# Routed rows in four classes instead of three, and the fourth lot of rows summed within the last three expert tiles

## What is computed

```python
xn = layernorm(x) * gamma + beta
logits = xn @ Wr + br                       # 8 experts
top_vals, top_idx = top_k(logits, 2)
w = softmax(top_vals)
for e in range(8):
    h = gelu(xn @ W1[e] + b1[e])            # 256 -> 512
    y += (h @ W2[e] + b2[e]) * w_full[:, e] # 512 -> 256
out = x + y
```

## Time and profile before

| what | value |
|---|---|
| median of three runs | 1207.3 us |
| lowest and highest of the three | 1204.22 and 1209.26 us |
| the profiled execution's own time | 1203.97 us |
| its span in the trace | 1202.2 us |
| PE busy | 1143.5 us, 95% of the span |
| DVE busy | 700.4 us, 58% |
| ACT busy | 418.6 us, 35% |
| POOL busy | 227.3 us, 19% |
| DMA | 105.98 MB, mean 88 GB/s |

### The profile page before, as it was taken

The page is one execution under the profiler, slowest core; times in us unless marked ns, Lnnn a source line. Parts: engine busy times, 40 slices in busy tenths (PEclk is TensorE's granted clock), DMA queues, the critical chain, the costliest instruction groups (busy, mean ns, idle before and its releaser), DMA issues.

```text
span 1202.2 us, 26290 instructions
## 1 busy us (share of the span) xinstructions
PE 1143.5 (95%) x7856; PEld 810.2 (67%) x7856; DVE 700.4 (58%) x1425; ACT 418.6 (35%) x806; POOL 227.3 (19%) x279
## 2 busy tenths in 40 slices
PE   5798999999999999999999999999999999899993
PEld 3586777776566666666666666666666667799993
DVE  7898999994444433443155433443344586775666
ACT  1676656663100000000022102121122236677682
POOL 2000000000012121112100000000112236567762
PEclk8998999999999999999999999999999999999997
DMA  6111011013344424443334303331224323323377
GB/s 158 57 43 39 27 32 31 26 34 103 87 92 93 90 56 105 102 100 71 66 114 126 100 23 114 97 109 61 33 66 146 119 84 124 91 79 99 116 211 203
DMA packets 77196, 105.98 MB, mean 88 GB/s; under 512 B 13559, under 2 KB 62510, under 8 KB 76988
## 3 DMA queue, kind: packets, MB, share of 16 engines
q1 hardware_dynamic: 63997, 75.26, 21.0%
q0 software_dynamic: 11376, 25.55, 9.4%
q10 hardware_dynamic: 1740, 4.11, 1.4%
HBM read 77.00 MB, written 37.49 MB: 95 GB/s over the span
## 4 chain that ended last, share of the span: by engine, by line
PE 83%; DVE 9%; DMA 2%; issue 2%; ACT 2%; DVEq 1%; ACTq 0%; POOL 0%; SPq 0%; POOLq 0%
PE ps L2005 45%; PE ps L2059 11%; PE ps L1983 7%; PE ps L2173 5%; PE ps L1951 5%; PE ps L2187 5%; DVE v_b L1244 3%; PE ps L1919 1%; DMA h_ring<-h_dram 1%; PE ps L1930 1%; DVE adj L1151 1%; PE ps L2087 1%; PE ps L2107 1%; ACT v_b L1089 1%; DMA adj<-y_dram 0%
## 5 line engine op out<-in xcount | busy, mean ns | idle before, releaser
L2005 PE MATMUL ps<-v_a,adj 125*125 125x512 f16 x1375 | 297.3, 379 | 0.0
L2005 PE MATMUL ps<-v_b,adj 125*125 125x512 f16 x1250 | 270.2, 379 | 1.5 <-DVE v_b L1269 1.5
L2005 PEld LDWEIGHTS ps<-v_a,adj 125*125 (+1 forms) x1375 | 187.6, 136 | 109.0
L2005 PEld LDWEIGHTS ps<-v_b,adj 125*125 x1250 | 170.6, 136 | 100.9 <-issue 2.0
L964 ACT ACTIVATE t_hi<-ps,cinv 125x256 f32<-125x256 f32 x125 | 59.2, 474 | 457.0 <-PE ps L2005 404.0
L1251 DVE SCALAR_TENSOR_TENSOR t_hi<-ps,cinv,t_hi 125x256 f32<-125x256 f32 x125 | 60.3, 483 | 240.7 <-ACT t_hi L964 240.7
L1244 DVE TENSOR_TENSOR v_b<-v_b 125x2560 f16<-125x2560 f16 x125 | 180.2, 1487 | 3.4 <-PE ps L1951 2.9
L2059 PE MATMUL ps<-v_b,adj 125*125 125x512 f16 x625 | 139.8, 380 | 0.3 <-issue 0.3
L939 ACT ACTIVATE adj<-ps 125x625 f32 (+1 forms) x125 | 112.1, 906 | 66.0 <-PE ps L1951 65.0
L1983 PE MATMUL ps<-v_a,adj 125*125 125x512 f16 x500 | 123.4, 378 | 0.0
L2059 PEld LDWEIGHTS ps<-v_b,adj 125*125 125x125 f16 x625 | 83.4, 137 | 46.2 <-issue 0.7
(11 more groups left out here) (282 smaller groups left out, 986.2 us busy)
## 6 DMA issues: line engine op xcount, KB each, us to landing
h_ring<-h_dram SPq DMA_DIRECT2D x125, 125.0 KB
v_a<-L_ffn_W SPq DMA_DIRECT2D x32, 256.0 KB, 3.4
v_b<-L_ffn_W SPq DMA_DIRECT2D x32, 256.0 KB, 3.4
adj<-w_dram SPq DMA_DIRECT2D x16, 512.0 KB, 5.3
adj<-y_dram SPq DMA_DIRECT2D x8, 560.0 KB
w_dram<-w_hi SPq DMA_DIRECT2D x32, 128.0 KB, 1.9
hx_dram<-h_dram POOLq DMA_DIRECT2D x25, 125.0 KB, 2.4
hx_dram<-x POOLq DMA_DIRECT2D x25, 125.0 KB, 3.2
```

Source lines behind the costliest of these rows:

```text
L2005: last = te.matmul(ps[0:NP, u, :], of_tile(adj[0:NP, 0:ADJ], i, u, a * NP, NP), source[:, a, :], start=(a == 0), stop=(a == T - 1))
```

## The change

There are four classes, with edges at token rows 15, 20, 23 and 25, and their tiles end at 37, 47, 52 and 56. The lots stay six: (0,5), (5,10), (10,15), (15,20), (20,23), (23,25). LOT_AT is 44 instead of 45, so that lots 0 to 2 are summed at steps 44 to 55; lot 3 is summed in pieces of 3, 3 and 4 instructions at steps 56, 57 and 58, and only lots 4 and 5 after the loop. SP loads lot 3 behind `landed(1)`, and lot 4 behind `store(2)` and `landed(2)`; the last lot follows `landed(3)`.

```diff
-    CUT = 22
-    LOTS = [(0, 5), (5, 10), (10, TA), (TA, 20), (20, CUT), (CUT, T)]
-    LOT_CLASS = (0, 0, 0, 1, 1, 2)
-    CLASS_TILES = [(TOP * rows * NP + NE * 127) // 128 for rows in (TA, CUT, T)]
+    CUTS = (TA, 20, 23, T)
+    LOTS = [(0, 5), (5, 10), (10, TA), *zip(CUTS, CUTS[1:])]
+    CLASS_TILES = [(TOP * rows * NP + NE * 127) // 128 for rows in CUTS]
     NCLASS = len(CLASS_TILES)
-    LOT_AT = 45
-    assert CLASS_TILES[-1] == FT and LOT_AT + 12 <= FT + LAG
+    LOT_AT = 44
+    assert CLASS_TILES[-1] == FT and LOT_AT + 12 <= FT
...
             landed(1)
-            for n in (3, 4):
-                for k in range(TOP):
-                    load(n, k)
+            for k in range(TOP):
+                load(3, k)
             store(2)
             landed(2)
+            for k in range(TOP):
+                load(4, k)
+            landed(3)
             load(5, 0)
...
-            for t in (0, TA, CUT):
+            for t in (0, *CUTS[:-1]):
                 g.memset(seg[:, :, t:t + 1], 0.0)
...
-                act.dma_start(y_in[last][1][part], y_v[1, part, CUT:T, :]).then_inc(yc_in[last], 16)
+                act.dma_start(y_in[last][1][part], y_v[1, part, CUTS[-2]:T, :]).then_inc(yc_in[last], 16)
...
-                for c, (t0, t1) in enumerate(((TA, CUT), (CUT, T))):
+                for c, (t0, t1) in enumerate(zip(CUTS, CUTS[1:])):
...
                 if LOT_AT <= j < LOT_AT + 12:
                     n, piece = (j - LOT_AT) // 4, (j - LOT_AT) % 4
                     weighted(n, *((0, 3), (3, 5), (5, 8), (8, 10))[piece])
+                if FT <= j < FT + LAG:
+                    weighted(3, *((0, 3), (3, 6), (6, 10))[j - FT])
...
-            for n in range(3, len(LOTS)):
+            for n in range(4, len(LOTS)):
                 weighted(n, 0, TOP * (LOTS[n][1] - LOTS[n][0]))
...
-                    ends = (TA - 1, CUT - 1, T - 1)
+                    ends = [t - 1 for t in CUTS]
```

## The result

The changed kernel takes 1211.4 us in the median of 17 runs (1208.0 to 1215.2), the kernel before 1207.3 (1203.7 to 1210.6): a ratio of 1.0034, with a 95% interval from 1.0024 to 1.0044. That is 4.1 us more, within the range and within 0.5%, but three times the +1.3 us of the sum. A few executions of the later runs, of several of the kernels, took 1278 to 3092 us and are in no ratio.

What follows compares the result with a forecast made beforehand. TensorE was taken to bound the kernel nearly everywhere, except the plan (1020 to 1080 us) and the tail. Terms +2.8, +0.1, +0.4 and -2.0 gave +1.3 us, so 1208.6 us against the median of 1207.3; range 1204.0 to 1212.5.

Steps and rivals of the forecast that it cites:

- the sum: All terms together: +2.8 in the plan, +0.1 and +0.4 at the scatters, -2.0 at the last lot: +1.3 us.
- the 1.5 us that had 55%: The forecast of 1208.6 us as it stands, within 1.5 us: chance 55%.
- three rivals: Count matmuls hide (1206.9, 15%); lot 3 late (1211.6 with 3 us wait, 7%); last scatter late (1210.5, 13%).
- a sign of its own for being wrong: Wrong if PE ends less than 1.5 or more than 4 us later, or the tail from PE's end grows.
- (a): PE, step 7: 16 more count instructions, 38 for 22, cost 1.75 us, not hidden; bounds 0.1 and 1.75.
- the first rival: The count matmuls hide: PE's 1.75 us go into the 1.64 us idle before step 12; 1206.9 us, chance 15%.
- (b): DVE, steps 7 and 8: wider `places_b` instructions and a third L1610 add 0.48 us; bounds 0.3 and 0.7.
- (c): DVE, step 17: `experts_of` compares 32 ends instead of 24, adding 0.55 us in full; bounds 0 and 0.7.
- The tail: After PE's end: +0.1 and +0.4 us at the scatters, -2.0 at the smaller last lot (load, sums, store).
- the second rival: Lot 3 comes late, delaying the last results and scatters at step 56; 1211.6 us with 3 us wait, chance 7%.
- the third: The last scatter lands late, at 5.9 us, beside lot 4's load: 1.9 us more, 1210.5 us; chance 13%.
- Lot 4's sums: After the loop: six sums start about 1190.5, end near 1193, before lot 5 is there, so cost nothing.

Runs made afterwards that it cites:

- e5: The kernel before, unchanged, on the faster chip, profiled again: ratio 1.0008 (0.9997 to 1.0020).
- e7: The kernel before with lot 3 alone moved into the last three tiles (LOT_AT 44), three classes: ratio 1.0010 (0.9997 to 1.0023) to the kernel before.
- e6: The changed kernel run again, on the faster chip: ratio 1.0037 (1.0023 to 1.0051) to the kernel before.
- e1: The kernel before with 16 more small count instructions at step 7, 38 in all, on the slower chip: ratio 1.0034 (1.0016 to 1.0052) to the kernel before.
- e9: The kernel of e1 again, 16 count instructions added to the kernel before, on the slower chip: ratio 0.9998 (0.9976 to 1.0020).
- e2: The kernel before with 1.75 us of dense 16-bit matmuls added at the count matmuls, on the slower chip: ratio 1.0046 (1.0025 to 1.0068) to the kernel before.
- e10: The kernel of e2 again, 1.75 us of dense matmuls added to the kernel before: ratio 1.0040 (1.0018 to 1.0061).
- e11: The kernel of e3 again, the changed kernel with its count instructions in two stretches: ratio 0.9979 (0.9961 to 0.9998) to the kernel before.
- e3: The changed kernel with its 38 count instructions split, 18 at step 6 and 20 at step 7, slower chip: ratio 0.9973 (0.9950 to 0.9996) to the kernel before.
- e4: The changed kernel with counts batched, 20 instructions instead of 38, on the slower chip: ratio 0.9985 (0.9967 to 1.0002) to the kernel before.
- e8: The changed kernel with batched counts and the table of experts made in three pieces, faster chip: ratio 0.9992 (0.9980 to 1.0004) to the kernel before.
- e12: The kernel of e8 with the first planes multiplied at step 13 instead of 12, slower chip: ratio 0.9956 (0.9936 to 0.9975) to the kernel before.

## Why the prediction was right, and where its sum was wrong

The direction, the range and "within 0.5%" held, and three of four groups of terms came out near their sizes. But the time is 2.8 us above the 1208.6 that the sum gave, outside the 1.5 us that had 55%. And the prediction had set a sign of its own for being wrong, PE ending more than 4 us later, and it came: the last tile's matmuls begin at 1189.45 and not at 1182.19, 7.3 us later. The range was wide enough because of three rivals and the spread of the runs, and none of the rivals is what happened. That it took in the clock is luck.

**(a), the count matmuls, is where it failed.** Their own work was sized well: from 1032.69 to 1035.8 their starts are 0.11 us apart, as taken. That they are not hidden was right, too: the idle time before step 12 did not shrink but grew, from 1.64 to 2.10 us, by DVE's part, so the first rival is out. The step that failed is the price "with the pitch of the 22": the sum had nothing for the clock of the later ones among the small matmuls and of the tiles behind them. What is left of the +5.50 us without 1.75 and 0.48 is 3.3 us in both profiles of the changed kernel, and the fall measured 1.64 us in two of three profiles of the kernel before or its plan at that speed (e5, e7), which the profile that I worked from happened not to have. With 1.6 to 3.3 us more in the sum it would be 2.9 to 4.6 over the kernel before; by the ratios 4.1 and 4.5 were measured.

The mean granted clock of every execution tells more than the profiles. Of 40 executions of the kernel before on the chip of e5, only two reach the 0.987 of the profile that I worked from; 20 have 0.984, and the mean is 0.9836. The 26 of the changed kernel (result and e6) have 0.9816. A fall of 3.4 us is 0.0014 of such a span, so the changed kernel has an estimated 4.8 us more at the lower level in the mean, which at 1.64 us for 3.4 would be 2.3 us of the 4.1. With the 1.3 of the sum that makes 3.6. These means say nothing of where the falls lie, and they take in the tail, so it is an estimate of the size and no more.

The rows that were there could have warned: they are marked busy with a tiny operand of 8 columns. The Trainium skill, "TensorE: Matmul & The Clock Gate", section "What's actually happening", says that the low level is the default and that recent activity of PE is what lifts it. The traces agree as far as they go: with 38 small instructions in one stretch the clock was at 1.2 GHz for 6.8 us, from within them on, in all four profiles that have them (after, e6, e1, e9), 20 or 22 of them had 6.8 us only where PE was also stalled (e2, e10, e11), else 3.4 us or none (before, e3 to e5, e7, e8, e12). That it is the smallness of the work, and not the delay, is not shown by a clean test, because e2 and e10 were spoiled; so why the fall is longer stays open.

**(b) and (c), DVE's part,** came as priced: L1605 and L1608 0.40 and 0.41 us, the third L1611 0.32 more, together 0.48; L1645 and L1648 1.29 each for 1.01 and 1.00, which is 0.57 against 0.55, and PE's wait before step 20 grew from 0.78 to 1.36 us, the whole of it.

**The tail** gave 1.86 us where 1.5 was forecast: the load 1.16 less (0.8 forecast), the sums 0.80 (0.8), the store some 0.5 (0.4), the last scatter's landing 0.73 more (0.4), its issue 0.10 less (0.1 more). Nothing waited for lot 3: the second rival is out. The last scatter landed in 4.29 us and not in 5.9, so the third is out as a whole, though its mechanism took 0.3 us more than the term had. Lot 4's sums waited 2.74 us for its load and ended at 1200.86, before lot 5 had landed at 1203.0, as predicted. For the 256 KB less in the last load the rows had given 0.8 us and the figure of the Trainium skill, "DMA: Bandwidth & Descriptors", section "Anatomy of one DMA", 0.6; the 1.16 us measured are nearer to the first. That section is on transfers that GpSimd issues, and these go out on SP's and ACT's queues. e7 adds what the prediction did not say: the move of lot 3 is worth nothing by itself.

0.68 us between step 20 and the last tile were in no step. The prediction took that stretch as busy in every 20 us but for 0.06 us; the profile that it read has PE idle for 0.35 us at 1101.83 as well, for ACT. PE waits 0.52 us for a gather at 1154.87 (0.34 in e6) and 0.3 us more for DVE in front of the last tile; the cause of the gather's lateness is open. Open, too, is how often the kernel before has its fall at this place, since only profiles tell where a fall lies.

## What to carry to other kernels

A few small matmuls between dense ones are priced by their pitch (the time from one start to the next) only up to a point: look for the granted clock in the windows among and right behind them, at 1 or 2 us a row, and in more than one execution, since one profile may have the fall and the next not. A fall costs only where PE's work is waited for. Before adding work to an engine, look for a wait of that engine close by: the split put 18 instructions into one of 1.95 us. One wide small matmul can stand for many: here 10 did the work of 19. Before moving work out of a tail, look whether it stands on the chain there: 4 us of sums did not.

## What the runs showed of the hardware that was not expected

- Two chips differ by 3% on the same kernel (1207.5 and 1243.7 us), and only a small part of the difference is in the clock: from 1080 to 1180 us e1 does 1119 matmuls at a mean clock of 0.97, the kernel before on the faster chip 1376 at 1.00, and PE is busy for 88.7 us of the 100 in place of 99.6. On the slower one PE idles between the matmuls of the unrolled expert tiles, 0.2 to 1.2 us at a time, with nothing waited for. A lack of instructions at PE would look like this, but no run tested it.
- Idle time of 2 us on PE can be followed by a fall of the clock, and need not be: e8 had it behind the 2.10 us at step 12 (3.4 us at 0.5), the changed kernel, with the same idle time, did not; e5 had it behind 1.99 us at 1024.66.
- A fall can begin after the small matmuls are over: in e5 they end at 1034.96 and the clock falls at 1035.9, with dense matmuls between.
